# Expert weights fetched matrix by matrix instead of expert by expert

## The chip, the cores and the metric

One NeuronCore of a Trainium2 chip runs the whole layer as one program. The metric is device time in microseconds (us) from the start to the end of that program; lower is better. The engines are the tensor engine (PE, with its weight loads shown as PEld), the vector engine (DVE), the scalar engine (ACT), GpSimd (POOL) and the sync engine (SP), which here only starts DMA transfers. Each engine has its own instruction queue; they wait for each other through semaphores. Sixteen DMA engines move data between DRAM and the on-chip memory (SBUF).

## The reference, cut to what matters

The layer is attention followed by a mixture of experts, over 16 x 512 = 8192 tokens of width 256. Only the second half matters here:

```
xf = x.reshape(-1, H)                       # 8192 tokens, H = 256
w = weights of the 2 best of 8 experts, per token, from softmax(layernorm(xf) @ gate_w.T)
out = (silu(xf @ sWg) * (xf @ sWu)) @ sWd   # the shared expert
for e in range(8):
    out = out + w[:, e:e + 1] * ((silu(xf @ Wg[e]) * (xf @ Wu[e])) @ Wd[e])   # INTER = 512
```

Each expert has three matrices of 256 x 512 numbers: gate (Wg), up (Wu) and down (Wd).

## The kernel before, in words

The program runs in stages with a barrier between them: attention (with the splitting of the experts' weights beside it), routing, the shared expert with a scatter that sorts the token rows by expert into `xs_d` in DRAM, and last the expert stage, `expert_stage`, which is all that the change touches.

**Slots.** The sorted rows are cut into `NSLOT` = 135 slots of 128 rows. All rows of one slot belong to one expert; the table `slot_e` says which, and PE reads it at run time (`value_load`), so that the number of the expert, `e`, is a register and not a constant. An expert fills about 17 slots. Slots 0 to 2 and the last ones are written out; slots 3 to 130 are 32 passes of a loop over four slots (`over_slots`).

**What a slot does.** PE, in `step(s)`: the gate product of slot s (`gate`, tile `ps_ge`), the transposes of the hidden rows of slot s-1 (`turn_hidden`, `ps_h`), the down product of slot s-2 (`down`, `ps_ye`), the transposes of the token rows of slot s+1 (`turn_rows`, `ps_x`), and the up product of slot s (`up`, `ps_ue`). Each product is done in three parts: a 32-bit high part of the weights (`w_hi`) with two parts of the data, and a bfloat16 rest (`w_lo`) with one. ACT and DVE split and multiply what PE leaves.

**POOL and its queue.** In `step(s)` POOL first starts the load of the token rows of slot s+2 (`xr<-xs_d`), when the buffer is free; then it waits for `y_taken` of slot s-2 and for the landing of the output of slot s-3 (`y_stored`), and starts the indirect transfer that adds slot s-2's rows to the output (`out_dram<-y_e,to`). So the outputs go one at a time, and the load of rows for the next slot stands behind the output in POOL's queue.

**The weights.** The split weights lie in DRAM as `whi_d` and `wlo_d`. SP loads them for all eight experts, one expert after the other, while the first slots already run: two transfers (1536 KB for `w_hi`, 768 KB for `w_lo`), a wait for both, a count on `w_ready`, then the next expert. They all stay in SBUF; nothing is loaded twice. On PE only `gate` waits for them, for `w_ready >= e + 1`; `up` and `down` of the same expert come later in PE's queue and need no wait of their own.

Of the kernel before, what the change touches and what calls it, by code (L numbers as in the profile page):

```python
# [22 lines left out]
F32 = mybir.dt.float32  # L23
# [1468 lines left out]
def expert_stage(nc, ctx, sbt, whi_d, wlo_d, xs_d, out, ident, slot_e):  # L1492
# [4 lines left out]
    def sb(name, shape, dt=F32):  # L1497
        return sbt(ctx, name, shape, dt)

    def sem(name):  # L1500
        return ctx.enter_context(nc.semaphore(name))

    GU = KT * INTER
    w_hi = sb("w_hi", [P, NE, 3, GU], F32R)
    w_lo = sb("w_lo", [P, NE, 3, GU], BF16)
# [18 lines left out]
    w_loaded = sem("we_loaded")  # L1524
    w_ready = sem("we_ready")
# [23 lines left out]
    def over_slots(eng, step):  # L1549

        for s in range(3):
            step(Batch(0, s))
        with eng.Fori(0, (NSLOT - 7) // 4) as i:
            for s in range(3, 7):
                step(Batch(i, s, 4))
        for s in range(NSLOT - 4, NSLOT + 2):
            step(Batch(0, s))

    def exists(s):
        return s.at_least(0) and s.at_most(NSLOT - 1)  # L1560
# [4 lines left out]
    @block.sync  # L1565
    def _(sp):
        for e in range(NE):
            sp.dma_start(w_hi[:, e].bitcast(F32), whi_d[e].rearrange("p m k n -> p m (k n)")).then_inc(w_loaded, 16)
            sp.dma_start(w_lo[:, e], wlo_d[e].rearrange("p m k n -> p m (k n)")).then_inc(w_loaded, 16)
            sp.wait_ge(w_loaded, (e + 1) * 32)  # L1570
            sp.nop(nofuse=True).then_inc(w_ready, 1)

    @block.gpsimd
    def _(pool):
# [29 lines left out]
    @block.tensor  # L1604
    def _(pe):
        def expert(s):
            at = slot_e[0:1, s.off:s.off + 1] if s.fixed else slot_e[0:1, bass.ds(s.v, 1)]
            return pe.value_load(at, min_val=0, max_val=NE - 1)

        def product(bank, n, hi, lo, bf, m, e, ready, count):  # L1610

            width = GU // n
            w = [t[:, bass.ds(e, 1), m].rearrange("p o n -> p (o n)") for t in (w_hi, w_lo)]
            for at, (part, side) in enumerate(((hi, 0), (bf, 1), (lo, 0))):
                if ready:
                    pe.wait_ge(ready[at], count)
                for k in range(n):
                    mm = nc.tensor.matmul(bank, part[:, k], w[side][:, k * width:(k + 1) * width],  # L1618
                                          start=at == 0 and k == 0, stop=at == 2 and k == n - 1)
            return mm  # L1620

        def turn_rows(s):
            pe.wait_ge(x_loaded[s.par], (s.half() + 1) * 16)
            if s.at_least(1):
                for taken_by in (xh_ready, xl_ready):
                    pe.wait_ge(taken_by, s.v)
            for k in range(KT):
                mm = nc.tensor.transpose(ps_x[:, k], xr[:, s.par, k * P:(k + 1) * P], ident[:])  # L1628
            mm.then_inc(tx_ready, 1)

        def gate(s, e):

            pe.wait_ge(w_ready, e + 1)
            if s.at_least(1):
                pe.wait_ge(sg_ready, s.v)
            product(ps_g[:], KT, x_hi[:, s.par], x_lo[:, s.par], x_bf[:, s.par], 0, e,
                    (xh_ready, xb_ready, xl_ready), s.v + 1).then_inc(g_ready, 1)

        def up(s, e):
            if s.at_least(1):  # L1640
                pe.wait_ge(h_ready, s.v)
            product(ps_u[:], KT, x_hi[:, s.par], x_lo[:, s.par], x_bf[:, s.par], 1, e, None, 0).then_inc(u_ready, 1)

        def turn_hidden(s):
            pe.wait_ge(h_ready, s.v + 1)
            if s.at_least(1):
                for taken_by in (hh_ready, hl_ready):
                    pe.wait_ge(taken_by, s.v)
            for k in range(IT):
                mm = nc.tensor.transpose(ps_h[:, k], h[:, s.par, k * P:(k + 1) * P], ident[:])  # L1650
            mm.then_inc(th_ready, 1)

        def down(s, e):
            if s.at_least(2):
                pe.wait_ge(y_taken, s.v - 1)
            product(ps_y[s.par][:], IT, h_hi[:, s.par], h_lo[:, s.par], h_bf[:, s.par], 2, e,
                    (hh_ready, hb_ready, hl_ready), s.v + 1).then_inc(y_ready, 1)

        def step(s):
            if exists(s):  # L1660
                e = expert(s)
                gate(s, e)
            if exists(s.plus(-2)):
                e_down = expert(s.plus(-2))
            if exists(s.plus(-1)):
                turn_hidden(s.plus(-1))
            if exists(s.plus(-2)):
                down(s.plus(-2), e_down)
            if s.at_most(NSLOT - 2):
                turn_rows(s.plus(1))  # L1670
            if exists(s):
                up(s, e)

        turn_rows(Batch(0, 0))
        over_slots(pe, step)
# [105 lines left out]
```

## Time and profile before

| | us |
|---|---|
| median of the timed runs (3) | 2224.79 (2224.26 to 2225.31) |
| the profiled execution | 2222.39 |
| its span, first to last instruction | 2220.7 |
| busy in the span: PE | 1972.8 (89%) |
| busy: DVE, ACT, POOL | 1252.4, 1081.6, 789.4 |
| start of the first weight load of the expert stage | 1529.07 |

The times of the rows below count from the span's start. The expert stage is the last 690 us of it. A group of instructions is named by its line in the kernel, its engine and its tiles (written<-read). SPq is SP's queue starting transfers; PEldq is the part of PE that works through its instruction queue (register arithmetic, semaphore waits, branches) and hands the matrix instructions on.

### The profile page before, as it was taken

The page shows a single profiled execution, that of the slowest core. Times are in us where ns is not written, and L with a number is a line of the kernel's source. Part 1 is how long each engine was busy: PE and PEld are TensorE (multiplying, and loading weights), DVE is VectorE, ACT ScalarE, POOL GpSimd, SP SyncE. Part 2 cuts the span into 40 slices and gives each one's busy share as a digit, 9 for nine tenths or more (in the row PEclk, how much of TensorE's full clock was granted, in tenths as well). Part 3 has the DMA queues.
Part 4 walks back from the last instruction along what each step waited for, and adds up shares of the span by engine and source line. Part 5 has one row for each costly group of instructions (what it writes and reads, how often), then busy time and mean ns, then how long its engine had stood idle before and what let it go on. Part 6 is the DMA issues. An engine that isn't in the chain of part 4 may idle for free. (4 is left out here: it accounts for less than half of the span.)

```text
span 2220.7 us, 47761 instructions
## 1 busy us (share of the span) xinstructions
PE 1972.8 (89%) x14698; PEld 1300.3 (59%) x14767; DVE 1252.4 (56%) x3885; ACT 1081.6 (49%) x2354; POOL 789.4 (36%) x1150
## 2 busy tenths in 40 slices
PE   2789999999999999999983699997799999999997
PEld 1345445455444454444432588885577777777776
DVE  5556667766666766667635555552355454544544
ACT  1155555555555555555540455542355555555554
POOL 2033323333333333332330355520244444444443
PEclk9699999999999999999985799998999999999999
DMA  7134343344344344343310565544733333333332
GB/s 211 36 102 113 119 135 122 113 131 118 117 132 128 115 120 122 116 131 119 113 61 15 184 211 207 198 135 156 255 58 58 53 57 55 57 58 54 55 55 36
DMA packets 152032, 246.07 MB, mean 111 GB/s; under 512 B 28896, under 2 KB 90080, under 8 KB 150848
## 3 DMA queue, kind: packets, MB, share of 16 engines
q1 hardware_dynamic: 116352, 189.24, 27.2%
q0 software_dynamic: 32064, 53.44, 11.4%
q8 instruction: 91, 1.49, 0.3%
q10 hardware_dynamic: 3456, 1.34, 0.2%
q14 instruction: 69, 0.57, 0.1%
HBM read 111.89 MB, written 90.50 MB: 91 GB/s over the span
## 5 line engine op out<-in xcount | busy, mean ns | idle before, releaser
L631 DVE CUSTOM_DVE_ANT_0 ps_rows<-ps_rows,maskrow 128x512 f32<-128x512 f32 (+3 forms) x1024 | 484.4, 514 | 304.6 <-PE ps_rows L488 303.7
L576 ACT ACTIVATE probs<-ps_cols 128x512 f32<-128x512 f32 (+3 forms) x1024 | 392.0, 435 | 390.6 <-PE ps_cols L499 383.9
L488 PE MATMUL ps_rows<-ks,qs 32*128 32x512 f32 (+3 forms) x2048 | 426.4, 491 | 88.1 <-DVE mx L631 50.3
L495 PE MATMUL ps_cols<-qs,ks 32*128 32x512 f32 (+3 forms) x2048 | 419.5, 486 | 2.5 <-ACT probs L576 2.4
L1596 POOL DMA_INDIRECT out_dram<-y_e,to x135 | 215.5, 1596 | 369.6 <-DMA out_dram<-y_e,to 193.6
L750 POOL TENSOR_TENSOR pace<-eps 1x1 f32<-1x1 f32 x256 | 58.0, 227 | 781.4 <-ACT probs L576 781.4
L488 PEld LDWEIGHTS ps_rows<-ks,qs 32*128 32x128 f32 x2048 | 161.4, 187 | 296.1 <-DVE mx L631 245.6
L499 PE MATMUL ps_cols<-mT,ones_r 32*128 32x512 f32 (+3 forms) x1024 | 285.3, 551 | 0.0
L1723 DVE TENSOR_TENSOR h_lo<-ps_h,h_hi 128x512 fp32r<-128x512 f32 x135 | 93.3, 691 | 216.1 <-ACT h_hi L1698 215.6
L1692 ACT ACTIVATE sg_e<-ps_ge 128x512 f32<-128x512 f32 x135 | 80.7, 598 | 267.2 <-PE ps_ge L1618 267.2
L512 PE MATMUL ps_o<-probs,vt 128*32 128x512 f32 (+3 forms) x2048 | 192.9, 449 | 0.8 <-POOL probs L752 0.8
L1486 POOL DMA_INDIRECT xs_d<-row,pos x128 | 131.2, 1025 | 151.9 <-ACT row L1457 123.9
L495 PEld LDWEIGHTS ps_cols<-qs,ks 32*128 32x128 f32 x2048 | 154.9, 185 | 9.8 <-ACT probs L576 7.6
L752 POOL TENSOR_SCALAR_AFFINE_SELECT probs<-probs 128x512 f32<-128x512 f32 x256 | 159.9, 624 | 0.0
L631 DVE DVE_READ_ACCUMULATOR2_ANT mx<- 128x1 f32 x1024 | 144.7, 141 | 0.1
L1739 DVE TENSOR_TENSOR h_e<-sg_e,ps_ue 128x512 f32<-128x512 f32 x135 | 92.8, 688 | 73.3 <-PE ps_ue L1618 73.3
L499 PEld LDWEIGHTS ps_cols<-mT,ones_r 32*128 32x128 f32 x1024 | 99.7, 188 | 51.6 <-issue 31.9
L1587 POOL DMA_DIRECT2D xr<-xs_d x133 | 117.5, 883 | 18.8 <-DVE to L1748 17.6
L1618 PE MATMUL ps_ge<-w_hi,x_lo 128*128 x270 | 111.2, 493 | 0.0
L1618 PE MATMUL ps_ue<-w_hi,x_lo 128*128 x270 | 111.1, 493 | 0.0
L1062 PE MATMUL ps_g<-x2T,swg 128*128 128x512 f32 x384 | 99.3, 394 | 6.7 <-DVE x2T L1168 6.7
L1062 PE MATMUL ps_u<-x2T,swu 128*128 128x512 f32 x384 | 98.4, 392 | 0.0
(207 smaller groups left out, 3733.6 us busy)
## 6 DMA issues: line engine op xcount, KB each, us to landing
xs_d<-zrows SPq DMA_DIRECT2D x45, 408.0 KB, 2.9
xr<-xs_d POOLq DMA_DIRECT2D x135, 136.0 KB, 3.1
whi_d<-w_sh SPq DMA_DIRECT2D x16, 768.0 KB, 3.8
w_hi<-whi_d SPq DMA_DIRECT2D x8, 1536.0 KB
xn<-in_L_attn_x_dram SPq DMA_DIRECT2D x16, 512.0 KB, 4.5
ks<-k_lin SPq DMA_DIRECT2D x64, 128.0 KB, 2.8
ks<-k_tan SPq DMA_DIRECT2D x64, 128.0 KB, 3.8
qs<-q_lin SPq DMA_DIRECT2D x64, 128.0 KB, 2.4
```

Of the source, the lines that this page charges most:

```text
L488: mm = nc.tensor.matmul(ps_rows[bank_of(row_no(g, it, h))][:, 0:(it + 1) * P], qs[at:at + STRIP, d.par, g, it * P:(it + 1) * P], ks[at:at ...
L495: nc.tensor.matmul(ps_cols[bank_of(col_no(n, s, e))][:, jt * P:S], ks[at:at + STRIP, b.par, gc, jt * P:(jt + 1) * P], qs[at:at + STRIP, b. ...
L499: mm = nc.tensor.matmul(ps_cols[bank_of(col_no(n, s, e))][:, jt * P:S], ones_r[at:at + STRIP], mT[at:at + STRIP, gc % 2, jt * P:S], start= ...
L512: mm = nc.tensor.matmul(ps_o[2 * HD * h:2 * HD * (h + 1), jt * P:S], vt[:, b.par, jt, g * HG + h], probs[:, n % 2, h, jt * P:S], start=jt ...
L576: nc.scalar.activation(probs[:, n % 2, 2 * (1 - s) + e, jt * P:S], ps_cols[bank_of(col_no(n, s, e))][:, jt * P:S], ACT.Exp).then_inc(exp_d ...
L631: nc.vector.tensor_tensor_reduce(out=bank, in0=bank, in1=maskrow[:, (TT - 1 - it) * P:S], scale=1.0, scalar=LOWEST, op0=ALU.add, op1=ALU.m ...
L752: nc.gpsimd.affine_select(out=blk, in_=blk, compare_op=ALU.is_ge, fill=0.0, base=0, pattern=[[0, HG], [1, P]], channel_multiplier=-1).then ...
L1062: mm = nc.tensor.matmul(bank[i % 2][:], w[:, wp, k, i * P:(i + 1) * P], self.x2T[:, s.par, xp, k], start=at == 0 and k == 0, stop=at == 2 ...
L1486: nc.gpsimd.indirect_dma_start(xs_d[:, :], bass.IndirectOffsetOnAxis(ap=pos[:, t, r:r + 1], axis=0), row[q][:, r], None).then_inc(scattere ...
L1587: pool.dma_start(xr[:, s.par], rows_of(xs_v, s.plus(2))).then_inc(x_loaded[s.par], 16)
L1596: nc.gpsimd.indirect_dma_start(out_v, bass.IndirectOffsetOnAxis(ap=to[:, d.quad], axis=0), y[:, d.par], None, bounds_check=NT * P - 1, oob ...
L1618: mm = nc.tensor.matmul(bank, part[:, k], w[side][:, k * width:(k + 1) * width], start=at == 0 and k == 0, stop=at == 2 and k == n - 1)
```

## The change

SP loads one matrix at a time: for each expert gate, up and down, each as two transfers (512 KB of `w_hi`, 256 KB of `w_lo`), with the wait for both and a count on `w_ready` behind each. That makes 24 rounds of two transfers where there were 8. On PE, `gate` waits for `w_ready >= 3e + 1`, and `up` and `down` get waits of their own, for `3e + 2` and `3e + 3`. The bytes, the buffers and the layout in DRAM are the same.

```diff
         for e in range(NE):
-            sp.dma_start(w_hi[:, e].bitcast(F32), whi_d[e].rearrange("p m k n -> p m (k n)")).then_inc(w_loaded, 16)
-            sp.dma_start(w_lo[:, e], wlo_d[e].rearrange("p m k n -> p m (k n)")).then_inc(w_loaded, 16)
-            sp.wait_ge(w_loaded, (e + 1) * 32)
-            sp.nop(nofuse=True).then_inc(w_ready, 1)
+            for m in range(3):
+                sp.dma_start(w_hi[:, e, m].bitcast(F32), whi_d[e, :, m].rearrange("p k n -> p (k n)")).then_inc(w_loaded, 16)
+                sp.dma_start(w_lo[:, e, m], wlo_d[e, :, m].rearrange("p k n -> p (k n)")).then_inc(w_loaded, 16)
+                sp.wait_ge(w_loaded, (e * 3 + m + 1) * 32)
+                sp.nop(nofuse=True).then_inc(w_ready, 1)
...
         def gate(s, e):
 
-            pe.wait_ge(w_ready, e + 1)
+            pe.wait_ge(w_ready, e * 3 + 1)
...
         def up(s, e):
+            pe.wait_ge(w_ready, e * 3 + 2)
...
         def down(s, e):
+            pe.wait_ge(w_ready, e * 3 + 3)
```

SP's queue at the start of the expert stage, before:

```order
L1565 UNCONDITIONAL_BRANCH [waits barrier_Pool_Activation_PE_DVE_SP_release]
L1568 DMA w_hi<-whi_d 128x3072
L1569 DMA w_lo<-wlo_d 128x3072
L1568 DMA w_hi<-whi_d 128x3072 [waits we_loaded]
L1569 DMA w_lo<-wlo_d 128x3072
```

and of the change:

```order
L1565 UNCONDITIONAL_BRANCH [waits barrier_Pool_Activation_PE_DVE_SP_release]
L1569 DMA w_hi<-whi_d 128x1024
L1570 DMA w_lo<-wlo_d 128x1024
L1569 DMA w_hi<-whi_d 128x1024 [waits we_loaded]
L1570 DMA w_lo<-wlo_d 128x1024
L1569 DMA w_hi<-whi_d 128x1024 [waits we_loaded]
L1570 DMA w_lo<-wlo_d 128x1024
```

Each transfer is a third as long, and the wait (`we_loaded`) that stood once per expert stands once per matrix.

PE's queue in the loop, where the down product begins, before:

```order
L1650 MATMUL ps_h<-ident,h_e 128x128 [waits hl_ready,hh_ready,he_ready]
L1650 MATMUL ps_h<-ident,h_e 128x128 x3
L1618 ISA [waits hh_ready,ye_taken]
L1618 MATMUL ps_ye<-w_hi,h_hi 128x256
L1618 ISA
```

and of the change:

```order
L1652 MATMUL ps_h<-ident,h_e 128x128 [waits hl_ready,hh_ready,he_ready]
L1652 MATMUL ps_h<-ident,h_e 128x128 x3
L1656 ISA
L1619 ISA [waits hh_ready,ye_taken,we_ready]
L1619 MATMUL ps_ye<-w_hi,h_hi 128x256
L1619 ISA
```

One register instruction (L1656, which works out 3e + 3) is new, and the next one waits for one semaphore more.

PE's queue in the loop, where the up product begins, before:

```order
L1628 MATMUL ps_x<-ident,xr 128x128 [waits xl_ready,xh_ready,xe_loaded1]
L1628 MATMUL ps_x<-ident,xr 128x128
L1618 ISA [waits he_ready]
L1618 MATMUL ps_ue<-w_hi,x_hi 128x512
L1618 ISA
```

and of the change:

```order
L1629 MATMUL ps_x<-ident,xr 128x128 [waits xl_ready,xh_ready,xe_loaded1]
L1629 MATMUL ps_x<-ident,xr 128x128
L1641 REGISTER_ALU
L1619 ISA [waits he_ready,we_ready]
L1619 MATMUL ps_ue<-w_hi,x_hi 128x512
L1619 ISA
```

A register instruction (L1641) is new, and there are now two waits on register values ahead of this product, of which one takes a semaphore instruction to itself. In `gate` an addition (a REGISTER_ALU) becomes one ISA instruction that multiplies and adds. That makes three instructions more per slot in this queue and one that is longer.

## Rows read from the trace of the kernel before

**Rows 1.** DMA issues on the page: engine, count, KB each.

```profile
w_hi<-whi_d SPq DMA_DIRECT2D x8, 1536.0 KB
...
w_lo<-wlo_d SPq DMA_DIRECT2D x8, 768.0 KB
```

**Rows 2.** Timeline of SP, first and last of the eight loads of w_hi.

```profile
1529.07 0.34 SPq L1568 DMA_DIRECT2D w_hi<-whi_d  x1
...
1594.26 0.32 SPq L1568 DMA_DIRECT2D w_hi<-whi_d  x1
```

**Rows 3.** Timeline of PE, 1530 to 1611: start, length, idle before and releaser.

```profile
1536.66 0.69 PE L1628 MATMUL ps_x<-ident,xr 128*128 128x128 f32 x2 [10.98 <-DMA xr<-xs_d]
1538.95 1.22 PE L1618 MATMUL ps_ge<-w_hi,x_hi 128*128 x2 [1.60 <-SPq L1571]
...
1541.98 0.95 PE L1618 MATMUL ps_ue<-w_hi,x_hi 128*128 x2
...
1552.46 0.63 PE L1618 MATMUL ps_ge<-w_hi,x_hi 128*128 x2
...
1575.95 0.44 PE L1628 MATMUL ps_x<-ident,xr 128*128 128x128 f32 x2 [4.34 <-DMA xr<-xs_d]
...
1610.74 0.73 PE L1618 MATMUL ps_ge<-w_hi,x_hi 128*128 x2 [0.29 <-issue]
```

**Rows 4.** Windows: PE, PEld, DVE, ACT, POOL busy, clock, DMA share, GB/s.

```profile
1555.00:1605.00 50.00, 35.98 (x192) 25.85 (x193) 15.29 (x39) 16.84 (x34) 11.72 (x11) 0.90 0.80 274
...
1559.00:1562.00 3.00, 2.93 (x23) 2.48 (x22) 1.54 (x3) 2.45 (x5) 1.70 (x2) 1.00 0.99 397
...
1700.00:1800.00 100.00, 99.29 (x616) 76.55 (x625) 50.09 (x126) 52.13 (x104) 45.84 (x42) 1.00 0.33 56
```

**Rows 5.** Issue to landing, 1525 to 1610: first tile xr, then tile out_dram.

```profile
DMA to landing us min/median/max: 2.7/7.0/7.8
...
DMA to landing us min/median/max: 3.8/8.0/8.6
```

**Rows 6.** Issue to landing, 1700 to 1900: first tile xr, then tile out_dram.

```profile
DMA to landing us min/median/max: 2.5/3.0/3.4
...
DMA to landing us min/median/max: 3.2/3.8/3.9
```

**Rows 7.** Timeline of POOL while the weights load: two outputs in a row.

```profile
1567.08 1.59 POOL L1596 DMA_INDIRECT out_dram<-y_e,to  x1 [6.38 <-PE ps_x L1628]
...
1576.45 1.60 POOL L1596 DMA_INDIRECT out_dram<-y_e,to  x1 [7.18 <-PE ps_x L1628]
```

**Rows 8.** Timeline of POOL after the weights: two outputs in a row.

```profile
1803.00 1.59 POOL L1596 DMA_INDIRECT out_dram<-y_e,to  x1 [2.54 <-DMA out_dram<-y_e,to]
...
1807.95 1.59 POOL L1596 DMA_INDIRECT out_dram<-y_e,to  x1 [2.74 <-DVE y_e L1731]
```

**Rows 9.** Timeline of PE, three gate products in a row.

```profile
1855.64 0.62 PE L1618 MATMUL ps_ge<-w_hi,x_hi 128*128 x2
...
1860.44 0.63 PE L1618 MATMUL ps_ge<-w_hi,x_hi 128*128 x2
...
1865.24 0.62 PE L1618 MATMUL ps_ge<-w_hi,x_hi 128*128 x2
```

**Rows 10.** Line 1553 (the loop), 1857 to 1860: duration ns, first and last start.

```profile
L1553 PEldq COMPARE_BRANCH  x1: 215/215/215, 1858.4 to 1858.4; - x1
```

**Rows 11.** Lines 1616 and 1618, 1859.55 to 1860.3; line 1648, 1861 to 1862.

```profile
L1616 PEldq ALU_OP  x1: 32/32/32, 1859.8 to 1859.8; - x1
...
L1618 PEldq FUSED_REGOPS  x4: 42/46/51, 1859.9 to 1860.3; - x4
...
L1648 PEldq EVENT_SEMAPHORE  x1: 51/51/51, 1861.5 to 1861.5; - x1
```

**Rows 12.** Timeline of PEld behind the loop's branch.

```profile
1860.21 0.42 PEld L1618 LDWEIGHTS ps_ge<-w_hi,x_hi 128*128 128x128 f32 x2
...
1861.59 0.59 PEld L1650 LDWEIGHTS ps_h<-ident,h_e 128*128 128x128 f32 x4
```

## The prediction

> **What bounds the kernel now.** I read the page first, then only the expert stage, since nothing ahead of 1529 us changes: SP's timeline for the weight loads, PE's timeline and waits, the landings of the two transfers that POOL starts, and last PE's instruction queue. The reader is to see three stretches.
>
> First the start. PE stands still until the first rows are turned at 1536.66, after 10.98 us of idle time that a transfer of rows ends, and the first gate product starts at 1538.95, with the last 1.60 us of idle time ended by SP's count on the weights [rows 3]. Rows and weights are late together.
>
> Then the loading stretch. SP starts eight loads from 1529.07 to 1594.26, one per (1594.26 - 1529.07) / 7 = 9.31 us [rows 2]. While they run, rows take 7.0 us from issue to landing and an output 8.0 us; later 3.0 and 3.8 [rows 5, 6]. PE waits for rows again and again, 4.34 us at 1575.95 [rows 3]; it is busy 36 of 50 us, and its granted clock is 0.90 there [rows 4]. The gate product of slot 3 starts at 1552.46 and that of slot 11 at 1610.74 [rows 3]: eight slots in 58.28 us. The undisturbed slot takes 4.80 us [rows 9], so the stretch loses 58.28 - 8 x 4.80 = 19.9 us. The outputs set the pace: two of them start 9.37 us apart [rows 7], about the landing of 8.0 plus 1.
>
> Last, some 600 us of undisturbed slots: PE is busy 99 us of 100 [rows 4]. An output started at 1803.00 lands 3.8 later and the next starts at 1807.95 [rows 6, 8]. So POOL's chain (landing, then about 1 us) takes about 4.8 us too: it keeps up with PE, but has no room for a slower landing.
>
> **The change, part by part.** Bytes, matrix products and the traffic of rows and outputs stay. What changes is the grain of the loads, when the first slots may start, and what PE's queue has to work through.
>
> *1. The start.* One expert is 1536 + 768 KB = 2.36 MB [rows 1], at the 397 GB/s of a stretch with little but weights [rows 4] 5.9 us. Gate 0 started 9.9 us after the first issue; 4.0 us of that is not data. One matrix is 0.79 MB or 2.0 us, so its first product can start at 1529.07 + 4.0 + 2.0 = 1535.1, which is 3.9 us earlier. Its rows then have at most 2.0 us of weights ahead of them instead of a whole expert: 3.0 + 2.0 from an issue near 1529.6 is 1534.6, in time. Up 0 needs the second matrix, one round later (5.4 us by step 2), at 1540.5, against 1541.98 before [rows 3]; that is a gain of only 1.5. PE's queue is in order, so the transposes and gate 1 stand behind that wait. Down 0 needs the third matrix near 1546 and comes after that. The start is worth 1.5 to 3.9 us; I take 3.
>
> *2. The loading stretch.* A round now has 2.0 us of data. The rest of the old round is 9.31 - 5.9 = 3.4 us; in it is the time that a slot's own rows and output take on the DMA engines, 0.33 of 4.80 = 1.6 us [rows 4]. With one slot's transfers in each round a round takes 2.0 + 3.4 = 5.4 us, with none 2.0 + 1.8 = 3.8. I take 5.4, as the old rounds had one slot each; then the 24 rounds last 130 us, to 1659, instead of 75. The stretch is longer but milder. An output landed 4.2 us late behind 2.36 MB; behind a third of that, by proportion, 1.4. The outputs' pace is then 4.8 + 1.4 = 6.2 us if every output meets a matrix head on, and 4.8 if every one falls in a gap. SP now leaves a gap without weights after every matrix, so I take the middle, 5.5, close to the round, as outputs and rounds kept one pace before (9.37 and 9.31). From slot 3, at about 1549.5 with step 1, to 1659 that is 110 / 5.5 = 20 slots with 0.7 us each, 14 us. I take off 1.5 because rows are loaded two slots ahead, which covers the first outputs; no row prices that. The loss is 12.5 instead of 19.9: a gain of 7.4. The clock helps a little: waits of 0.7 us instead of 4 should leave it at 1.00.
>
> The bounds are no loss (gain 19.9) and 110 / 6.2 = 18 slots x 1.4 = 25 us (5 worse than before).
>
> The Trainium skill (DMA: Bandwidth & Descriptors, Anatomy of one DMA) gives a DMA about 2.0 us of fixed time plus its bytes at 436 GB/s, and advises batches of 1 MiB and more. By that a round of one matrix would take an estimated 3.8 us, the rule speaks for large loads when loading is what one waits for, and here it would put the end of loading near 1620. The rows give more than 2.0 us beside the data.
>
> *3. PE's queue.* Three instructions more per slot, each about 0.1 us from one start to the next (1859.8 to 1859.9) [rows 11], and one that is a little longer: 0.35 us a slot, 47 us over 135 slots. What matters is how much of it hides. The queue runs ahead of the matrix work. The loop's branch, 215 ns on its own [rows 10], stands between the gates of 1855.64 and 1860.44; they are 4.80 us apart, as are the next two without a branch [rows 9]. So an extra of about 0.4 us per pass is hidden now. But it has used up the cover in that slot: the register instruction of the gate product runs at 1859.9 and its weights load at 1860.21 [rows 11, 12], a lead of 0.3; the wait ahead of the transposes of the hidden rows runs at 1861.5, their load at 1861.59, a lead of 0.1, which is about the least that passing on takes. An extra 0.35 leaves the gate product about 0.15 late (0.35 less a lead of 0.2 beyond the least), and the transposes no more than that. I take 0.15 us once per pass of four slots, and nothing in the other three slots, where there is no branch. The loading stretch hides it (five passes), so 27 x 0.15 = 4 us lost. The bounds are 0 and 0.35 in each of 115 slots, 40.
>
> The landed semaphores themselves cost nothing after the start: expert 1 is wanted some 17 x 4.8 = 82 us after expert 0, and its third matrix is there after 6 rounds, 32 us.
>
> **The sum.** -3 - 7.4 + 4 = -6.4 us. The profiled execution of 2222.39 (span 2220.7, 1.7 around it) would become 2216.0. The median of the timed runs lies 2.4 above it, so I put 2224.8 - 6.4 = 2218.4, rounded to 2218.5.
>
> **The rivals.**
>
> *A. The stalls vanish.* For it: with 2.0 us of data in a round over half of the DMA time is free, and rows are ordered two slots ahead. Against: POOL's chain has no room, so any output that is late is a late slot. It would give -3 - 19.9 + 4.6 = -18.3, 2206.5. Chance 0.15. The skill's fixed cost, above, would speak for this one.
>
> *B. The longer stretch costs more than the short one.* Every output meets a matrix, 6.2 us a slot: 25 - 1.5 = 23.5 instead of 19.9 lost, -3 + 3.6 + 4 = +4.6, 2229.4. For it: outputs and rounds fell into one pace before. It decides from a pace of about 6 us on. Chance 0.15.
>
> *C. PE's queue becomes the bound in every slot* (this is the one that ends clearly slower). The place is the start of the gate and down products, the price up to 0.35 us in each of some 115 slots. It decides from a cover of less than 0.35 us in an ordinary slot. With 0.15 uncovered in each slot it is 17 us instead of 4, +6.9, 2231.7; with all of it +30, 2254. Against it: a branch of more than 0.2 us hides whole [rows 9, 10]. For it: PE is busy 99 of 100 us, so nothing lost is made good. Chance 0.15.
>
> *D. The terms cancel*: a pace of 5.8 us gives a loss of 19 x 1.0 - 1.5 = 17.5 and a sum near -1.4, 2223.4. Chance 0.13.
>
> **How the numbers follow.** The forecast has 0.42. About 0.2% (4.4 us) is what a measurement of this kernel can tell from no change. The forecast of -6.4 with its own range of -12 to -2 lies three quarters on the faster side and one quarter within: 0.32 and 0.10. A adds 0.15 to faster; D gives 0.11 to same and 0.02 to faster; B is split, 0.08 slower and 0.05 same, with 0.02 faster; C is 0.14 slower and 0.01 same. Faster 0.51, same 0.27, slower 0.22. The range of 2206 to 2232 takes in A's and C's nearer values and leaves out C's far end.
>
> **What the changed profile would show.** Step 1: gate 0 near 1535, up 0 with a wait that SP ends, near 1540.5. Step 2: rounds of 5.0 to 5.8 us, the last load near 1654; outputs landing in about 5 us; many small waits of PE for rows, no clock below 1.00. Step 3: undisturbed gates 4.80 us apart, except one in four that is 0.1 to 0.2 longer. Wrong would be: undisturbed slots that are all longer (C), no waits for rows at all (A), or a pace above 6 us while loading (B). The likeliest mistake is the pace in step 2, which is chosen between two bounds and not read from a row.

## The result and the profile after

The changed kernel takes 2200.05 us (median of 5 timed runs, 2197.91 to 2204.27) against 2224.79 us for the kernel before (2224.17 to 2226.56): a ratio of 0.9891, 95% interval 0.9876 to 0.9905. That is 24.7 us faster. Of the runs further down, 1 and 3 each had one execution at a far lower granted clock (2844.83 and 3252.09 us), which their ratios leave out. The prediction was 2218.5 with a range of 2206 to 2232; the direction was right, and the time lies outside the range.

The stage accounting below uses the profiled execution of each kernel and counts from the stage's own first weight load, because stages that the change doesn't touch took another time in that execution: the first load starts at 1534.46 here and at 1529.07 before [rows 2]. SP's timeline of the changed kernel, loads of w_hi only: the first two, three in a row from the middle, and the last of 24:

```profile
1534.46 0.34 SPq L1569 DMA_DIRECT2D w_hi<-whi_d  x1
1539.08 0.32 SPq L1569 DMA_DIRECT2D w_hi<-whi_d  x1
...
1562.11 0.32 SPq L1569 DMA_DIRECT2D w_hi<-whi_d  x1
1566.60 0.32 SPq L1569 DMA_DIRECT2D w_hi<-whi_d  x1
1572.27 0.32 SPq L1569 DMA_DIRECT2D w_hi<-whi_d  x1
...
1644.36 0.32 SPq L1569 DMA_DIRECT2D w_hi<-whi_d  x1
```

23 rounds take 1644.36 - 1534.46 = 109.9 us, 4.78 each, where eight had taken 9.31 each. PE's timeline, gate products of slots 0, 3, 11 and 30 and two late ones, with the first turned rows and the first up product:

```profile
1539.37 0.69 PE L1629 MATMUL ps_x<-ident,xr 128*128 128x128 f32 x2 [8.30 <-DMA xr<-xs_d]
1540.73 1.21 PE L1619 MATMUL ps_ge<-w_hi,x_hi 128*128 x2 [0.67 <-ACT x_hi L1686]
...
1543.76 1.07 PE L1619 MATMUL ps_ue<-w_hi,x_hi 128*128 x2
...
1554.33 0.62 PE L1619 MATMUL ps_ge<-w_hi,x_hi 128*128 x2
...
1592.74 0.63 PE L1619 MATMUL ps_ge<-w_hi,x_hi 128*128 x2
...
1683.93 0.62 PE L1619 MATMUL ps_ge<-w_hi,x_hi 128*128 x2
...
1861.53 0.63 PE L1619 MATMUL ps_ge<-w_hi,x_hi 128*128 x2
...
1866.33 0.62 PE L1619 MATMUL ps_ge<-w_hi,x_hi 128*128 x2
```

Slots 3 to 11 take 1592.74 - 1554.33 = 38.41 us, eight times 4.80; before they took 58.28 [rows 3]. Slots 3 to 30 take 129.60, which is 27 times 4.80, so nothing at all is lost while the weights load. In the kernel before, the gate product of slot 30 stood here in the same timeline:

```profile
1702.04 0.39 PE L1618 MATMUL ps_ge<-w_hi,x_hi 128*128 x1
```

1702.04 - 1552.46 [rows 3] = 149.58, so 20.0 us were lost. The landings while the weights load, first tile xr, then tile out_dram of the changed kernel, answer to [rows 5]:

```profile
DMA to landing us min/median/max: 2.3/3.0/4.4
...
DMA to landing us min/median/max: 3.8/3.8/4.5
```

Outputs land in 3.8 us instead of 8.0, rows in 3.0 instead of 7.0: what they take without any weights [rows 6]. POOL's timeline, three outputs in a row while weights load, answers to [rows 7]:

```profile
1564.13 1.59 POOL L1597 DMA_INDIRECT out_dram<-y_e,to  x1 [2.48 <-DVE y_e L1734]
...
1568.93 1.60 POOL L1597 DMA_INDIRECT out_dram<-y_e,to  x1 [2.60 <-DMA out_dram<-y_e,to]
...
1573.76 1.59 POOL L1597 DMA_INDIRECT out_dram<-y_e,to  x1 [2.60 <-DMA out_dram<-y_e,to]
```

They start 4.8 us apart instead of 9.37. Set against SP's rows above, they start 2.0, 2.3 and 1.5 us behind the first load of their round; all 20 outputs of the loading stretch start 1.4 to 2.4 us behind one. The windows of the changed kernel (PE, PEld, DVE, ACT, POOL busy, clock, DMA share, GB/s):

```profile
1555.00:1605.00 50.00, 49.65 (x312) 38.50 (x315) 24.14 (x63) 26.29 (x52) 23.62 (x22) 1.00 0.84 221
1700.00:1800.00 100.00, 99.30 (x618) 76.62 (x626) 49.98 (x125) 52.82 (x105) 45.59 (x43) 1.00 0.32 56
```

The DMA engines are busier in the loading stretch than before (0.84 against 0.80 [rows 4]) while fewer bytes move in a second (221 against 274 GB/s), and yet nobody waits: PE is busy 49.65 of 50 us, at a granted clock of 1.00 instead of 0.90.

**Where the time went.** From the first weight load to the end of the span: 691.6 us before, 668.1 after, 23.5 less. Gate product 3 starts 23.39 us after the first load before and 19.87 after it now: 3.5 us from the start. Slots 3 to 30 give 20.0 us. Slots 30 to 50 take 96.0 us in both, and so it goes on to the end. 3.5 + 20.0 is the whole of it. The timed runs differ by 1.2 us more; the stages that the change doesn't touch vary by more than that (run 9).

### The profile page after: what moved, and what is told of

The parts are those of the page before. It is cut to its first block and busy times, and to the rows that moved or that the text cites. A ratio compares the mean times of both kernels' runs of the same rounds, so it can differ in the third digit from the quotient of the medians.

```text
span 2202.6 us, 48214 instructions
## 1 busy us (share of the span) xinstructions
PE 1975.4 (90%) x14698; PEld 1300.5 (59%) x14767; DVE 1252.1 (57%) x3885; ACT 1081.8 (49%) x2354; POOL 790.8 (36%) x1150
## 5 line engine op out<-in xcount | busy, mean ns | idle before, releaser
L1588 POOL DMA_DIRECT2D xr<-xs_d x133 | 111.6, 839 | 15.6 <-DVE to L1751 14.0
L1619 PE MATMUL ps_ue<-w_hi,x_lo 128*128 x270 | 109.9, 488 | 0.0
```

The costliest lines, as they stand in the source:

```text
L1588: pool.dma_start(xr[:, s.par], rows_of(xs_v, s.plus(2))).then_inc(x_loaded[s.par], 16)
```

## The experiments

Before the first of them the question was why an output that met 2.36 MB of weights landed 4.2 us late and one that meets 0.79 MB is not late. **The main theory**: what counts is how many bytes of weights SP has in flight when the small transfer is issued; it gets through only between them. **Rivals**: the length of the rows (a row of w_hi is 12 KB for a whole expert and 4 KB for one matrix, and a shorter row lets a small transfer in sooner); and the pause without weights that SP leaves between a landing and the next load. On PE's side the question was how much room its queue has left. Nothing is left out of the computation in any run. All times are medians, and each ratio is against the kernel before as it was timed beside that run (2224.44 to 2226.1 us); the outputs' landings are counted from the first load of w_hi to 5 us after the last; "lost" is the start of gate product 30 less that of gate product 3, less 27 x 4.80; "stage" runs from the first weight load to the end of the span.

**1. Small transfers, one wait per expert.** Against the kernel before; PE's waits are as before.

```diff
-            sp.dma_start(w_hi[:, e] ...); sp.dma_start(w_lo[:, e] ...)
-            sp.wait_ge(w_loaded, (e + 1) * 32)
+            for m in range(3):
+                sp.dma_start(w_hi[:, e, m] ...); sp.dma_start(w_lo[:, e, m] ...)
+            sp.wait_ge(w_loaded, (e + 1) * 96)
```

> The loads are cut by matrix (six transfers per expert, the same short rows of 4 and 2 KB per partition as in the change), but there is one wait per expert as before, so 2.36 MB are in the queue at once; the tensor engine waits as before. Theory 1, what holds up rows and outputs is the amount of weights that is queued ahead of them: outputs land in 7 to 8 us, rounds of about 9.3 us, 2220 to 2227 us. Theory 2, it is the length of one row of the transfer (12 KB), since the engines take turns row by row: outputs land below 5.5 us while loading, 2202 to 2212 us.

Measured: 2220.29 us, ratio 0.9979 (0.9969 to 0.999). Lost 16.0 of 20.0; stage 687.7. The landings of the outputs while loading:

```profile
DMA to landing us min/median/max: 3.8/7.1/8.9
```

The same 24 small pairs, but with 2.36 MB in flight, give back only 4 us. The short rows, with six transfers where there were two, are a small part of the gain; the rest comes with the wait behind each matrix (run 2).

**2. The rounds of the change, but PE waits once per expert.** SP loads as in the change, but counts on `w_ready` once per expert; PE is as before.

```diff
+            for m in range(3):
+                sp.dma_start(w_hi[:, e, m] ...); sp.dma_start(w_lo[:, e, m] ...)
+                sp.wait_ge(w_loaded, (e * 3 + m + 1) * 32)
             sp.nop(nofuse=True).then_inc(w_ready, 1)
```

> SP loads matrix by matrix with a wait behind each, as in the change; the tensor engine waits only in the gate product, for the whole expert, as before, and its queue is the old one. Theory 1 and 2 both: the waits for rows are gone, the start is as late as before or later (three rounds, first gate product about 13 us after the first load against 9.9 before and 6.3 in the change), so 7 us of the gain is lost: 2204 to 2209 us. If the tensor engine's own waits cost anything after the start, undisturbed slots are shorter here than in the change; I expect 4.80 us in both.

Measured: 2205.85 us, 0.9913 (0.9892 to 0.9934). Lost 0.0; outputs land in 3.7/3.9/4.6 us; stage 675.0. PE's timeline at the start, turned rows and gate product 0:

```profile
1533.97 0.69 PE L1629 MATMUL ps_x<-ident,xr 128*128 128x128 f32 x2 [8.20 <-DMA xr<-xs_d]
...
1542.56 1.22 PE L1619 MATMUL ps_ge<-w_hi,x_hi 128*128 x2 [7.89 <-SPq L1572]
```

SP's part alone wins the whole loading stretch. PE's part wins the start: here gate 0 waits 7.89 us for the third matrix, and gate 3 comes 26.76 us after the first load, not 19.87. So with rounds the finer waits of PE are worth 6.9 us, 3.4 of them only because three rounds take longer than one large one did.

**3. Rounds with long rows.** Three rounds per expert, cut by partitions (48, 48, 32), so that rows keep their 12 and 6 KB.

```diff
+            for r, (f, l) in enumerate(((0, 48), (48, 96), (96, 128))):
+                sp.dma_start(w_hi[f:l, e] ...); sp.dma_start(w_lo[f:l, e] ...)
+                sp.wait_ge(w_loaded, (e * 3 + r + 1) * 32)
```

> Three rounds per expert, each with a wait, but cut by partitions (48, 48, 32), so each row stays 12 KB and 6 KB long; the tensor engine waits as before for the whole expert. Theory 1 (amount queued): as e2, outputs land in 3.8 to 4.6 us, 2204 to 2210 us. Theory 2 (length of a row): outputs land in 5 to 6.5 us and slots take 5.5 us or more while loading, 2212 to 2225 us.

Measured: 2238.21 us, 1.0051 (1.0031 to 1.0071). Lost 25.4. It does not tell row length from amount, because the transfers themselves became slow. A window of 5 us within the round of an expert's first 48 partitions, which lasts 8.4 us from its first load to the next; columns as above:

```profile
1588.50:1593.50 5.00, 5.00 (x35) 3.88 (x33) 2.23 (x4) 2.73 (x7) 2.20 (x2) 1.00 0.96 156
```

The DMA engines are 0.96 busy and move 156 GB/s, against 397 with whole tiles [rows 4]; rounds last 6.37 us in the mean. With the rate changed as well, this run says nothing of the row length and is read no further.

**4. Two rounds per expert with long rows.** The kernel before with a wait between w_hi (1.57 MB, rows of 12 KB) and w_lo (0.79 MB).

```diff
             sp.dma_start(w_hi[:, e] ...).then_inc(w_loaded, 16)
+            sp.wait_ge(w_loaded, e * 32 + 16)
+            sp.nop(nofuse=True)
             sp.dma_start(w_lo[:, e] ...).then_inc(w_loaded, 16)
```

> Two rounds per expert, each with a wait: the whole w_hi (1.57 MB in rows of 12 KB), then the whole w_lo (0.79 MB in rows of 6 KB); all 128 partitions in each; the tensor engine waits as before. Theory 1, the amount that is queued in one piece decides: between one round and three rounds, outputs land in about 5 to 6 us, the stretch from the third to the eleventh gate product loses 5 to 15 us (19.9 before, 0 in the change), 2210 to 2222 us. Theory 2, long rows alone hold the small transfers up: as before, 19 us lost, 2222 to 2228 us.

Measured: 2215.08 us, 0.9953 (0.9937 to 0.9969). Lost 8.6; stage 682.7. Landings of the outputs:

```profile
DMA to landing us min/median/max: 3.8/5.1/6.7
```

**5. The same rounds with short rows.** Gate and up together (1.57 MB), then down (0.79 MB), each matrix as its own pair; PE's waits as before.

```diff
+            for m in range(3):
+                sp.dma_start(w_hi[:, e, m] ...); sp.dma_start(w_lo[:, e, m] ...)
+                if m:
+                    sp.wait_ge(w_loaded, (e * 3 + m + 1) * 32)
+                    sp.nop(nofuse=True)
```

> Two rounds per expert: gate and up matrices together (1.57 MB), then the down matrix (0.79 MB), in the short rows of the change (4 and 2 KB); the tensor engine waits as before. The same amounts per round as in the kernel that loads w_hi and then w_lo, which lost 8.6 us between the third and the thirtieth gate product. Theory 1 alone (amount queued): 7 to 10 us lost again, 2212 to 2217 us. If the length of a row adds to it: 2 to 7 us lost, 2207 to 2213 us. Theory 2 alone (only long rows hold up): nothing lost, as in the kernel with three rounds and the old wait, 2205 us.

Measured: 2215.26 us, 0.9959 (0.994 to 0.9978). Lost 8.1; stage 682.5. Landings of the outputs:

```profile
DMA to landing us min/median/max: 3.8/5.0/6.5
```

Runs 4 and 5 have equal rounds and rows of a third the length, and come out alike: 8.6 and 8.1 lost. At these sizes the row length is worth nothing that shows.

**6. Two matrices always in flight.** The change, with SP waiting for the matrix before last (two semaphores in turn).

```diff
-                sp.wait_ge(w_loaded, (e * 3 + m + 1) * 32)
+            if r >= 1:
+                sp.wait_ge(w_loaded[(r - 1) % 2], ((r - 1) // 2 + 1) * 32)
```

> The change, but a matrix is asked for when the one before the last has landed, so two are always in flight (1.57 MB) and there is no gap between them. Theory 1 (the amount queued, and with it the gap that a wait leaves): rounds of 2.5 to 3 us, all loaded in 65 to 75 us, outputs land in 6 us and more, 10 to 20 us of the gain is lost, 2210 to 2220 us. Theory 2 (length of a row, which is 4 KB here): outputs land below 5 us, the gain stays, 2200 us.

Measured: 2212.02 us, 0.9937 (0.9918 to 0.9957). Lost 11.7; stage 680.0, 11.9 more than the change. Landings of the outputs:

```profile
DMA to landing us min/median/max: 3.8/5.8/6.6
```

The rounds come every 3.0 us and the weights are all there after 72 us instead of 115. Loading sooner is worth nothing; 1.57 MB in flight costs 11.7.

**7. One matrix in flight, a shorter pause.** w_hi and w_lo of a matrix take turns: each is asked for when the one of its own kind before it has landed, so that never more than 0.79 MB is in flight, and seldom nothing.

```diff
+            if r:
+                sp.wait_ge(w_loaded[0], r * 16)
+                sp.nop(nofuse=True)
             sp.dma_start(w_hi[:, e, m] ...).then_inc(w_loaded[0], 16)
+            if r:
+                sp.wait_ge(w_loaded[1], r * 16)
...
             sp.dma_start(w_lo[:, e, m] ...).then_inc(w_loaded[1], 16)
```

> The bytes and waits of the change, but w_hi and w_lo of a matrix are rounds of their own, staggered: the next w_hi is asked for when the last w_hi has landed, while w_lo is still under way, and the same for w_lo. Never more than one matrix (0.79 MB) is queued, but there is hardly a gap without weights. Theory 1a, the amount queued decides: outputs land in 3.8 to 4.6 us and nothing is lost between the third and the thirtieth gate product (0 to 2 us), 2197 to 2203 us. Theory 1b, it is the gap behind each matrix into which outputs and rows fit: all loaded in 80 to 95 us, outputs land in 5 us or more, 6 to 12 us lost, 2206 to 2214 us.

Measured: 2203.45 us, 0.9899 (0.9871 to 0.9927). Lost 5.2; stage 673.4. Landings of the outputs:

```profile
DMA to landing us min/median/max: 3.8/4.0/5.6
```

The median output is on time, and some are 1.8 late. But this is no run without a pause. Loading was to be done in 80 to 95 us and took 111, against 115 in the change, since each transfer still waits for the one before it. In the packets of the two traces weights move in 82% of the loading time here and in 70% in the change, and stand still 0.9 us at a time instead of 1.5; in run 6 they hardly stand still at all. And 5.1 of the 5.2 us are lost by gate product 13 (1602.85), while the weights go on loading to 1641 in the same way (windows as above):

```profile
1549.95:1603.00 53.05, 49.94 (x301) 36.44 (x301) 24.25 (x60) 25.19 (x50) 22.01 (x20) 1.00 0.83 215
1603.00:1636.00 33.00, 33.00 (x210) 25.06 (x208) 16.46 (x42) 17.38 (x35) 15.46 (x14) 1.00 0.84 218
```

Amount in flight, DMA share and rate are alike in both windows, and only the first loses time. What also differs is where the outputs fall. The first three start 0.1 us before, 1.0 behind and 0.8 before the nearest load and land in 5.5 to 5.6 us; from 1603 on they land in 3.9 in the median. So that a shorter pause costs 5.2 us is not shown.

**8. Large rounds with a longer pause.** Run 5, with a transfer of 64 bytes and a wait for it behind each round, which adds a pause of about 1.2 us.

```diff
                     sp.nop(nofuse=True)
+                    sp.dma_start(pause[:], whi_d[0, 0:1, 0, 0, 0:16]).then_inc(paused, 16)
+                    sp.wait_ge(paused, (e * 2 + m) * 16)
+                    sp.nop(nofuse=True)
```

> The kernel with the gate and up matrices in one round and the down matrix in the next, and behind each round one tiny load into a spare tile with a wait, a pause of about 2 us more without weights. Theory 1a (amount queued): each large round still holds up one output, 6 to 9 us lost between the third and the thirtieth gate product as without the pause (8.1). Theory 1b (the gap): less than 4 us lost. The pauses make loading longer by 16 x 2 us, and the start by 2 to 4 us, in both.

Measured: 2233.16 us, 1.0034 (1.002 to 1.0048). Lost 28.0, against 8.1 without the pauses; stage 705.1. Landings of the outputs, and SP's timeline, first load of each of four experts, with POOL's outputs of the last three rounds (the round between these two loads starts at 1592.31):

```profile
DMA to landing us min/median/max: 5.4/6.4/8.0
```

```profile
1554.83 0.32 SPq L1571 DMA_DIRECT2D w_hi<-whi_d  x1
...
1569.72 0.32 SPq L1571 DMA_DIRECT2D w_hi<-whi_d  x1
...
1584.03 0.32 SPq L1571 DMA_DIRECT2D w_hi<-whi_d  x1
...
1598.31 0.32 SPq L1571 DMA_DIRECT2D w_hi<-whi_d  x1
```

```profile
1584.27 1.59 POOL L1604 DMA_INDIRECT out_dram<-y_e,to  x1 [4.42 <-DMA out_dram<-y_e,to]
...
1592.10 1.60 POOL L1604 DMA_INDIRECT out_dram<-y_e,to  x1 [5.64 <-DVE to L1756]
...
1598.52 1.59 POOL L1604 DMA_INDIRECT out_dram<-y_e,to  x1 [4.20 <-PE ps_x L1636]
```

Both theories missed: one had 6 to 9 us lost, the other less than 4, and it is 28.0. That more pause lets more outputs through is refuted: while weights load, not one output lands in under 5.4 us. An expert's two rounds now last 14.9, 14.3 and 14.3 us, and two outputs start in that time, one in each round. Read against SP's rows, eleven of twelve outputs start within 0.7 us of the first load of a round, where those of run 5 start 1.4 to 2.5 us behind it. Taken output by output (start in POOL's timeline, landing by tile out_dram), this sorts the two causes:

| run | outputs start, us behind the first load of their round | land in us, 1.57 MB in the round | land in us, 0.79 MB in the round |
|---|---|---|---|
| 8 | -0.7 to 0.5 | 6.8 to 8.0 (6 outputs) | 5.4 to 5.9 (5) |
| 5 | 1.4 to 2.5 | 5.3 to 6.5 (6) | 3.8 to 4.7 (6) |
| the change | 1.4 to 2.4 | | 3.8 to 4.5 (20) |

Both count. At a like start the larger round holds an output up by some 1.6 us more; and in a round of the same size an output that starts together with the loads lands some 1.6 us later than one that starts 1.4 us or more behind them. No run moved the start alone, so this is read from traces and not set by an experiment.

**9. The change once more.** Twelve empty instructions per slot were put into PE's queue.

```diff
+            for _ in range(6):
+                pe.nop(nofuse=True)
```

> The change, with six empty instructions more ahead of the waits of the up and of the down product in the tensor engine's queue, twelve per slot, about 0.1 us each. Theory 3, the queue has cover left in every slot: at most 0.1 us per slot, below +10 us against the change (2200 to 2210 us). Theory 4, the change had just used up the cover behind the loop's branch (a lead of 0.13 us is left there): about 1.1 us late once in four slots, +30 us or more, 2230 us and up.

Measured: 2195.5 us, 0.986 (0.9836 to 0.9884). The empty instructions leave no record in the trace; whether they ran at all isn't shown. The run behaves as the changed kernel: stage 668.5 (668.1), lost 0.0. As a test of the queue it says nothing. It says how well the change repeats: 2200.05 and 2195.5, while the stage agrees within 0.4 us; the rest varies in the untouched stages.

**10 to 12. Work for PE's queue that does appear.** The change plus one more wait on a semaphore per slot (about 0.12 us); plus one more read of the expert's number ahead of `up` (about 0.65 us with what belongs to it); plus a second one ahead of `down` (about 1.3 us).

```diff
+            if exists(s):                        # run 10
+                pe.wait_ge(w_ready, e * 3 + 1)
+                pe.nop(nofuse=True)
...
+            expert(s)                            # run 11: ahead of up; run 12: ahead of down too
```

> The change with one more semaphore wait per slot in the tensor engine's queue, ahead of the transposes of the token rows, about 0.12 us. One read more (0.65 us) had cost 0.47 us per slot, so some 0.2 us of cover should be left per slot in the change: undisturbed slots of 4.80 us, 2197 to 2202 us. If the cover was gone already: 4.90 us per slot, +13 us.

> The change, and in the tensor engine's queue the number of the expert is read once more ahead of every up product (a read, two register operations and a check, about 0.65 us per slot). Theory 3, the queue has cover in every slot: the undisturbed slot stays 4.80 us and the time within 2 us of the change. Theory 4, the cover behind the loop's branch is used up (0.13 us left in the change): 0.3 to 0.5 us once in four slots, +10 to +15 us.

> As the kernel with one more read per slot, and a second one ahead of every down product, so about 1.3 us more per slot in the tensor engine's queue than in the change. Theory 3: still hidden, 4.80 us per slot. Theory 4: the gate product behind the loop's branch at least 0.8 us late, and the other slots late too, +30 to +90 us.

Run 10: 2198.77 us, 0.99 (0.9877 to 0.9923), stage 668.7 (668.1). Its gate products in PE's timeline are still 4.80 apart:

```profile
1860.45 0.63 PE L1619 MATMUL ps_ge<-w_hi,x_hi 128*128 x2
...
1865.26 0.63 PE L1619 MATMUL ps_ge<-w_hi,x_hi 128*128 x2
```

Run 11: 2260.65 us, 1.0168 (1.0144 to 1.0191), stage 731.1. Its gate products in PE's timeline, and the read in PE's queue (number, duration in ns):

```profile
1864.62 0.71 PE L1619 MATMUL ps_ge<-w_hi,x_hi 128*128 x2 [0.32 <-issue]
...
1870.00 0.72 PE L1619 MATMUL ps_ge<-w_hi,x_hi 128*128 x2
...
1875.12 0.73 PE L1619 MATMUL ps_ge<-w_hi,x_hi 128*128 x2
...
1880.28 0.73 PE L1619 MATMUL ps_ge<-w_hi,x_hi 128*128 x2
```

```profile
L1609 PEldq TENSOR_LOAD <-slot_e x114: 297/301/408, 1700.0 to 1898.8; - x114
```

(731.1 - 668.1) / 135 = 0.47 us more per slot. Run 12: 2358.77 us, 1.0605 (1.0583 to 1.0626), stage 825.8, which is 1.17 us per slot, so the second read costs 0.70. If the first is as long, 0.70 - 0.47 = 0.23 us of it was hidden: that much cover the change leaves in a slot. Once it is gone, the second read counts in full. Two of its gate products:

```profile
1872.92 0.73 PE L1619 MATMUL ps_ge<-w_hi,x_hi 128*128 x2
...
1878.95 0.73 PE L1619 MATMUL ps_ge<-w_hi,x_hi 128*128 x2
```

**13. A better start.** The change, with the first two tiles of rows asked for by SP ahead of the weights instead of by POOL, and the first two matrices asked for together.

```diff
+        for r in range(2):
+            sp.dma_start(xr[:, r], xs_v[r]).then_inc(x_first[r], 16)
+        load(0)
+        load(1)
...
-        for r in range(2):
-            pool.dma_start(xr[:, r], xs_v[r]).then_inc(x_loaded[r], 16)
```

> The change with a faster start: SP, not POOL, loads the first two tiles of token rows, ahead of the weights, and the first two matrices are asked for together; from the fourth matrix on one at a time as in the change. First gate product 5.2 to 5.6 us after the first load instead of 6.3, third gate product 18.5 to 19.3 instead of 19.9; the rest as in the change: 0.5 to 1.3 us less than the change, 2197 to 2200 us, too little to tell from it by the times alone. Rival: the rows are ready earlier but the first weights land as late as before, and nothing moves.

Measured: 2199.43 us, 0.9904 (0.9885 to 0.9923). SP's timeline, first loads, and PE's, first turned rows and gate product 0:

```profile
1528.62 0.83 SPq L1570 DMA_DIRECT2D xr<-xs_d  x2
1529.50 0.42 SPq L1573 DMA_DIRECT2D w_hi<-whi_d  x1
```

```profile
1530.80 0.69 PE L1643 MATMUL ps_x<-ident,xr 128*128 128x128 f32 x2 [5.56 <-DMA xr<-xs_d]
...
1534.12 1.21 PE L1630 MATMUL ps_ge<-w_hi,x_hi 128*128 x2 [2.64 <-SPq L1586]
```

The rows come sooner and then the weights end the wait: gate 0 starts 5.5 us after SP's first issue instead of 6.27, and the stage with the row loads is 667.4 against 668.1. The timed runs can't tell 0.7 us; this is no better version that can be measured.

**All loads side by side** (in flight: most bytes of weights asked for and not landed; the 8.0 before is that of [rows 5], and 8.3 when counted as in the other rows):

| run | in flight, MB | outputs land, median us | lost, us | gate 3 after the first load | stage |
|---|---|---|---|---|---|
| before | 2.36, long rows | 8.0 | 20.0 | 23.39 | 691.6 |
| 1 | 2.36, short rows | 7.1 | 16.0 | 23.10 | 687.7 |
| 4 | 1.57, long rows | 5.1 | 8.6 | 25.87 | 682.7 |
| 5 | 1.57, short rows | 5.0 | 8.1 | 26.08 | 682.5 |
| 6 | 1.57, hardly a pause | 5.8 | 11.7 | 19.72 | 680.0 |
| 7 | 0.79, shorter pause | 4.0 | 5.2 | 19.82 | 673.4 |
| the change | 0.79 | 3.8 | 0.0 | 19.87 | 668.1 |
| 2 | 0.79 | 3.9 | 0.0 | 26.76 | 675.0 |
| 8 | 1.57, longer pause | 6.4 | 28.0 | 28.80 | 705.1 |

## Why the prediction was wrong

**The step that failed is step 2, the loading stretch.** It said: "behind a third of that, by proportion, 1.4", then took "the middle, 5.5" for the outputs' pace, and so 12.5 us lost where 0.0 were. One of its bounds, "no loss (gain 19.9)", was the truth to 0.1 us. Two things in the step were wrong, the share of outputs that meet a matrix and the room in POOL's chain.

The middle was the one that cost the 12.5 us. It stood for outputs of which half meet a matrix head on. In the change none does: all 20 start 1.4 to 2.4 us behind the first load of their round and land in 3.8 us in the median, 4.5 at most. That is the bound "4.8 if every one falls in a gap", and the pace was 4.8. The price of the other bound, 1.4 us late head on, was not far off: in run 8 outputs that start together with a round of 0.79 MB land in 5.4 to 5.9 us, 1.6 to 2.1 late. What it had wrong is where the outputs fall. The prediction had named the reason, a round with 2.0 us of data and a gap behind it, and priced it at one half.

The room in the chain was the other. The slots' chain had room for a late output of a few tenths: the largest landing of 4.5 us plus about 1 is more than 4.80, and still no slot is late. So POOL's chain has no room for a landing that is late every time, but it has for a single one; that this is because outputs and rows are ordered ahead of their use is how I read the queues, and no run took that lead away. "I take off 1.5 because rows are loaded two slots ahead" was this term. And the rounds: 5.4 was foreseen, 4.78 came, from 4.3 to 5.8 us. That is near the slot's 4.80, as 9.31 had been close to the outputs' 9.37; but in run 11, with slots of 5.3 us, they average 4.91, and in run 12, with slots of 6.0, 4.75, so the rounds do not follow the slots in general. That rounds and outputs fell into one pace before was read as a sign of collisions; here it goes with none. What sets the point at which an output starts in its round, behind the loads in the change and in runs 2 and 5, together with them in run 8, stays open, so that it came out well in the change is not explained.

The amount matters beside it, and not in proportion: the loss is 20.0 us with 2.36 MB, 8.1 to 11.7 with 1.57 MB in runs 4 to 6 but 28.0 in run 8, and 0.0 to 5.2 with 0.79 MB.

The Trainium skill (DMA: Bandwidth & Descriptors, Queues, rings and completion order) says that an engine takes its queues' packets in turn. The trace before shows 8.0 us against 3.8 all the same, and runs 1 and 5 show that rows of a third the length change this little (16.0 for 20.0 lost, and 8.1 for the 8.6 of run 4). The same page's section on bandwidth advises batches of 1 MiB and more. For the loading itself that agrees with the kernel before, done in 75 us against 115 in the change; but run 6 is done in 72 with the small transfers, two matrices in flight. And nobody waits for loading behind the first slots: every run with more bytes in flight was slower than the change. The 3.8 us a round that the prediction estimated from the Trainium skill (DMA: Bandwidth & Descriptors, Anatomy of one DMA) was too short: the shortest took 4.3. The formula there is a fit for transfers that GpSimd issues, and these are SP's.

**Step 1, the start, held.** Foreseen were 3 us, between 1.5 and 3.9; measured 3.5 at gate 3 and 3.6 at gate 0. Its parts were off: up 0 has no wait at all and starts 9.3 us after the first load, not 11.4, because a round took 4.6 us and not 5.4; and gate 0 comes 6.27 and not 6.0 after it, since the rows' landing ends PE's 8.30 us of waiting. The matrix was there in time, the rows not, and run 13 turns this round for 0.7 us. What the rounds alone would have cost the start, 3.4 us, PE's finer waits give back with 3.5 on top (run 2).

**Step 3, PE's queue, was mis-sized:** "27 x 0.15 = 4 us lost", measured 0. The gate products behind the loop's branch are 4.80 us apart like the others. PE's queue and weight loads behind the branch in the changed kernel:

```profile
L1553 PEldq COMPARE_BRANCH  x1: 215/215/215, 1859.8 to 1859.8; - x1
```

```profile
L1619 PEldq FUSED_REGOPS  x2: 51/51/51, 1861.2 to 1861.3; - x2
```

```profile
1861.30 0.19 PEld L1619 LDWEIGHTS ps_ge<-w_hi,x_hi 128*128 128x128 f32 x1
```

The lead of the gate product's register instruction over its weight load sank from 0.3 [rows 11, 12] to 0.1 us, so the lead shrank as foreseen; what was not foreseen is that no gate product is late by it. Runs 10 to 12 give the size: 0.12 us more is free, and of a read of 0.70 us 0.23 is hidden. So the cover in a slot is now about 0.23 us (if the two reads cost the same); with the 0.35 us that the change put in, it was near 0.6 before (an estimate), where the prediction had taken about 0.2 behind the branch.

**The rivals.** A ("the stalls vanish") is what happened, with -3.5 - 20.0 + 0 where it had -3 - 19.9 + 4.6. It had a chance of 0.15. What spoke against it, POOL's chain without room, didn't hold. B did not happen in the change; its mechanism exists, and run 8 shows it, with nearly every output head on and 28.0 lost. C's mechanism is shown by runs 11 and 12, at a dose beyond that of the change. D needed a pace of 5.8 us, and the slots kept 4.80. The clock came back to 1.00, as foreseen.

**The account.** From -6.4 to the -23.5 of the two profiled executions' stages are 17.1 us: 12.6 belong to step 2 (the 12.5, and 0.1 that the loss before was larger), 4 to step 3 and 0.5 to step 1. The floor of the range, 2206, is about A's sum, which kept 4.6 us for PE's queue; without that term its own bounds gave -3 - 19.9 = -22.9, 2201.9.

## What to carry to other kernels

When small transfers on which the engines wait share the DMA engines with a bulk load that nobody waits for yet, limit what the bulk load has in flight, and look at the landing times of the small ones and at where in a round they start, not at the bandwidth: here 0.79 MB at a time, with a wait behind each, cost nothing and 2.36 MB cost 20 us. Let the consumer wait for the piece and not for the whole, or the start pays for the finer rounds. And don't take the middle between "no loss" and "full loss" where two sequences run at one pace: every meeting can then fall at the same point, and the change lay at one end, run 8 near the other.

## What the runs showed of the hardware

- A small transfer is held up by large ones on another queue according to what is in flight and to when it starts. Outputs that take 3.8 us alone landed in 8.0 with 2.36 MB in flight, in 5.0 to 6.4 in the median with 1.57 MB, and in 3.8 to 4.0 with 0.79 MB. Started within 0.7 us of the loads they took 5.4 to 5.9 us even in a round of 0.79 MB (run 8), and 3.8 to 4.7 from 1.4 us behind them (run 5).
- Rows of 12 or 4 KB made 4 us of difference in the loss at 2.36 MB and 0.5 at 1.57 MB.
- In a round that loads the first 48 of 128 partitions the DMA engines were 0.96 busy and moved 156 GB/s (run 3), where whole tiles moved 397 at 0.99.
- A pause of about 1.2 us behind each round made the loss grow from 8.1 to 28.0 us: how rounds fall against the outputs can matter more than how long they are.
- The read of a number from SBUF by PE's queue takes 0.30 us, and costs a slot about 0.70 with what belongs to it; empty instructions leave no record in the trace.
